# One feed-forward step of the odd chunks moved from slot 0 to slot 14 of the even chunk's middle

## What is computed

```python
x = L0_xattn(x, ctx, ctx, bias, bias, ...)   # 16 heads, 64 context tokens, layer norm
# L1 block
h1 = ln(x);  x = attn(h1, h1, 8-bit rounded q, k, v and weights) @ wo + bo + x    # 1024 keys
h2 = ln(x);  x = attn(h2, ctx, 8-bit rounded q, k, v and weights) @ wo + bo + x   # 64 keys
h3 = ln(x)
a, g = split(h3 @ ff_w1 + ff_b1)             # 2048 columns each
x = a * gelu(g) @ ff_w2 + ff_b2 + x
```

## Time and profile before

| | before |
| --- | --- |
| median of 3 runs | 3263.64 us (3263.4 to 3265.72) |
| the profiled execution, its own time | 3268.94 us |
| its span, first to last instruction | 3267.1 us |
| mean granted TensorE clock | 0.937 of full |
| TensorE matmul busy | 2906.6 us, 89% |
| VectorE busy | 2171.1 us, 66% |
| POOL busy | 1775.2 us, 54% |
| ScalarE busy | 1468.4 us, 45% |

### The profile page before, as it was taken

How to read it: one execution, slowest core, us unless ns; L and a number is a source line. 1 busy time by engine, 2 the same in 40 slices (tenths; PEclk the granted TensorE clock), 3 DMA queues, 4 the chain that set the end, 5 groups by cost and what they waited for, 6 DMA issues and landing times.

```text
span 3267.1 us, 50805 instructions
## 1 busy us (share of the span) xinstructions
PE 2906.6 (89%) x19712; PEld 2128.6 (65%) x19712; DVE 2171.1 (66%) x3591; ACT 1468.4 (45%) x2130; POOL 1775.2 (54%) x1698
## 2 busy tenths in 40 slices
PE   6677786898899989899889999899989999899998
PEld 6565554556677656667677656666767756666777
DVE  3467696784665686796675587687574588688521
ACT  5332462673333364474323365375324266275321
POOL 3456484785555185485455186386364277377321
PEclk9888756999999999999999999899999999999999
DMA  8744103335443314324443412333453322232444
GB/s 266 251 180 161 51 16 116 118 122 200 167 167 120 135 40 155 127 98 157 131 178 99 161 53 106 127 111 146 141 186 116 148 78 100 89 143 93 166 168 155
DMA packets 199758, 436.40 MB, mean 134 GB/s; under 512 B 94944, under 2 KB 103392, under 8 KB 182368
## 3 DMA queue, kind: packets, MB, share of 16 engines
q1 hardware_dynamic: 199520, 433.15, 37.1%
HBM read 363.38 MB, written 65.54 MB: 131 GB/s over the span
## 4 chain that ended last, share of the span: by engine, by line
PE 58%; POOL 16%; DVE 11%; issue 6%; ACT 4%; DMA 2%; SPq 1%; POOLq 0%; DVEq 0%; ACTq 0%
PE psum L1756 17%; PE psum L1758 15%; PE psum L1757 15%; POOL w1b L1011 6%; PE psum L2052 4%; PE psum L2040 2%; POOL rec L1006 2%; DVE e L1644 2%; PE psum L2066 1%; POOL u_lo L1030 1%; POOL x L925 1%; POOL fw_lo L1018 1%; ACT e L1315 1%; POOL w_lo L913 1%; DMA fw_lo<-pieces 1%
## 5 line engine op out<-in xcount | busy, mean ns | idle before, releaser
L1315 ACT ACTIVATE e<-e,nb 128x1024 f32<-128x1024 f32 x512 | 588.3, 1149 | 335.0 <-DVE e L1644 331.8
L1644 DVE TENSOR_SCALAR_CACHE_REDUCE e<-psum,nscale 128x1024 f32<-128x1024 f32 x512 | 652.8, 1278 | 76.8 <-POOL w1b L1011 54.4
L1011 POOL TENSOR_SCALAR w1b<-e,rec 128x1024 f16<-128x1024 f32 x512 | 574.6, 1122 | 95.2 <-POOL rec L1006 56.5
L1756 PE MATMUL psum<-h_hi,fw_hi 128*128 128x512 f32 x1024 | 458.1, 447 | 39.8 <-DVE h_lo L1401 14.8
L1657 DVE TENSOR_SCALAR w1T<-psum 128x1024 bf16<-128x1024 f16 x512 | 352.1, 688 | 96.6 <-PE psum L2052 93.1
L2052 PEld LDWEIGHTS psum<-ident,w1b 128*128 128x128 f16 x4096 | 255.8, 104 | 243.9 <-issue 131.5
L2052 PE MATMUL psum<-ident,w1b 128*128 128x128 f16 x4096 | 347.1, 233 | 74.9 <-POOL w1b L1011 46.1
L1757 PE MATMUL psum<-h_lo,fw_hi 128*128 128x512 f32 x1024 | 410.8, 401 | 0.0
L1758 PE MATMUL psum<-h_hi,fw_lo 128*128 128x512 f32 x1024 | 410.7, 401 | 0.0
L919 POOL TENSOR_TENSOR rstd<-ve,mhalf 128x1 f32<-128x1 f32 x128 | 88.5, 691 | 401.4 <-DVE ve L1507 401.4
L1756 PEld LDWEIGHTS psum<-h_hi,fw_hi 128*128 128x128 f32 x1024 | 196.3, 192 | 158.9 <-issue 98.4
(11 more groups left out here) (187 smaller groups left out, 6192.6 us busy)
## 6 DMA issues: line engine op xcount, KB each, us to landing
fw_hi<-pieces SPq DMA_DIRECT2D x168, 512.0 KB, 3.3
fw_lo<-pieces SPq DMA_DIRECT2D x168, 512.0 KB, 4.3
w_hi<-kept SPq DMA_DIRECT2D x45, 1024.0 KB, 4.9
w_lo<-kept SPq DMA_DIRECT2D x45, 1024.0 KB, 7.2
mixed<-mixed SPq DMA_DIRECT2D x32, 1024.0 KB, 5.1
fbias<-in_fside_Bx16xSxS SPq DMA_DIRECT2D x64, 256.0 KB, 3.0
unsplit<-in_L_xattn_ff_w SPq DMA_DIRECT2D x24, 512.0 KB, 5.0
pieces<-fw_hi SPq DMA_DIRECT2D x24, 512.0 KB, 2.7
```

What stands on the lines that cost most here:

```text
L1011: pool.tensor_scalar(w1b[u % NH][:], e1[u % NE][:], rec1[:, u % 8:u % 8 + 1], HALF, ALU.mult, ALU.add).then_inc(w1_ready.sem, 1)
L1315: act.activation(e1[s % NE][:], e1[s % NE][:], ACT.Exp, bias=nb1[:, s % NE:s % NE + 1], scale=-1.0, accum_out=sum1[:, s % 8:s % 8 + 1]).th ...
L1644: emptied_bank(dve.tensor_scalar(e1[s % NE][:], psum[:, i:i + 2, :].rearrange("p i n -> p (i n)"), nscale[:, 0:1], LARGEST, ALU.mult, ALU.min,
L1756: pe.matmul(o, s_hi, m_hi, start=first, stop=False)
```

## The change

In the list of the middle's slots for `FROM_A`, slot 0 is taken out and slot 14 put in. There are 14 steps in the middle, as before.

```diff
-FROM_A = host_quarters(8, 18, (0, 1, 2, 3, 4, 6, 10, 11, 12, 13, 15, 17, 19, 21))
+FROM_A = host_quarters(8, 18, (1, 2, 3, 4, 6, 10, 11, 12, 13, 14, 15, 17, 19, 21))
```

## The result

| | before | after |
| --- | --- | --- |
| median of 5 runs | 3263.64 us (3262.29 to 3267.55) | 3279.8 us (3276.44 to 3281.66) |
| the profiled execution, its own time | 3268.94 us | 3279.31 us |
| its span | 3267.1 us | 3277.5 us |
| mean granted TensorE clock | 0.937 | 0.937 |

A forecast was written before the change was run, and what follows sets the result against it. TensorE, busy 89% of the span, was taken as the bound. Terms -0.7 + 4.5 + 0.3 + 1.0 gave +5.1 us a middle, +15.3 for three: 3284.2 us profiled, less 5.3, is 3279.0 us, range 3269 to 3287.

The forecast's parts named there:

- (1): Even middle's entry, slot 0: TensorE idles 2.1 us for the split, yet the first output projection starts earlier; -0.7 us.
- (2): Slot 14: a3[3] runs wholly within TensorE's 6.15 us of idle time before the second turning; costs 0.
- (3): Slot 15: d3[0] waits for POOL's `u_lo`, now behind tile 3's scaling and 16-bit copy; +4.5 us, the main term.
- (5): Entry: the clock may fall after the new idle time, slowing a step and a projection; +1.0 us, ends 0 and 2.9.
- (4): Around slot 15: the clock is low when d3[0] starts, perhaps somewhat longer; +0.3 us, ends -1.9 and +1.5.
- (6): SP's load queues: pieces for a3[2] and d3[0] are issued later but arrive in time; 0 us, other end 2 us late.
- Rival A: Around slot 15: `u_lo` precedes tile 3's scaling and the clock stays high; 7.8 us faster, 3255.8 us; 6%.
- Rival B: Next self-attention's entry: its 1.88 us of idle time absorbs part of the delay; 3269.3 us with no clock loss; 10%.
- C: More than forecast: a3[2]'s piece lands 2 us late, or the clock is low at both places for long; 3286.5 us; 10%.
- D: Slot 14: the step doesn't fit and pushes the turning as well, because of the bank; 3287.7 us; 3%.

The follow-up runs named there:

- Experiment 7: The kernel before with slot 0's step moved into the self-attention (19 hosted steps there, 13 in the middle); ratio 1.0029.
- Experiment 6: The kernel before with a self-attention step (17 left there) put into slot 14 and d3[0] in slot 16; 3262.61 us, ratio 0.9989.
- experiment 4: The changed kernel with POOL's `u_lo` of a3[3] ahead of its scaling of tile 3 in the even middles; 3278.61 us, ratio 1.0034.
- experiment 1: The kernel before with slot 13's step moved to slot 14, slot 0 keeping its step; 3275.96 us, ratio 1.0028.
- experiment 2: The changed kernel with d3[0] moved from slot 15 to slot 16, behind the turning of tile 2; 3263.84 us, ratio 0.9994 to the kernel before.
- experiment 9: The kernel before with slot 1's step moved to slot 14, d3[0] staying in slot 15; 3270.0 us, ratio 1.0008.
- experiment 5: The changed kernel with nine unread matmuls in the entry's idle time; 3279.68 us, ratio 1.0037 to the kernel before.
- experiment 8: The kernel before with slot 1's step moved to slot 14 and d3[0] in slot 16; 3256.44 us, ratio 0.9975.

## Why the prediction was right

Forecast +15.3 us, 3279.0 us; measured 3279.8 us. By its steps, for each middle:

- **(1) The entry**, -0.7 us: measured -0.5 (2.28 us idle, not 2.1; the projection starts 0.25 us after `ht_lo` ends, where I took 0.1). Experiment 7 shows the same 2.28.
- **(2) Slot 14**, 0: measured 0.1 in chunk 4, where the clock didn't fall: 59.56 us to the second turning against 59.50. Experiment 6 shows a step more at no cost.
- **(3) The wait**, +4.5 us: measured +4.47 in all three. That POOL's order makes it is shown by experiment 4 (1.7 us back from that alone), and that it makes the kernel slower by experiments 1 and 2, and by experiment 9 in the middles. It does so because slot 0's step gives nothing back, terms (1) and (5); the 2.7 us a middle of slot 1's step would have paid for more than half of it (experiment 9).
- **(4) The clock around d3[0]**, +0.3 us, between -1.9 and +1.5: measured +0.4, -0.5 and +0.7 up to the turning of tile 2, and in chunk 2 another +0.4 behind it.
- **(5) The clock at the entry**, +1.0 us: measured +1.65, 0 and +1.65, mean 1.1. It is all or nothing at a place, and I forecast its mean. One of the two neighbours was read too narrowly. There is a fourth odd middle, chunk 1's, where TensorE idles 2.49 us before the second turning, at 849.10 us, and the granted clock is 0.51 for the 3.4 us behind it. So even in the odd middles the clock doesn't always stay high.
- **(6) The queues**, 0: no wait for a piece was seen. Here SP issues the loads for a3[2] after slot 10, and a3[2] starts without a wait for them (its idle time of 1.40 us ends with `gate`, as in the earlier trace rows).

The sum is 5.5 us a middle against 5.1 forecast. That the time agrees to 1 us is partly luck: the ratio's interval is 7.5 us wide, and the middles' 16.5 us stand against 10.4 us in the two profiled spans. Two terms, the clock's, were guesses between far ends, and their means came out near.

Rival A (clock kept high) failed where it was said to: `u_lo` came behind tile 3's scaling, and the clock was at 0.50 when d3[0] started. Rival B (the delay taken back at the next self-attention's entry) had the price of the forecast's low end, so only the trace can rule it out. It does: after the change TensorE idles 1.88 us at that entry in all three places, the same as in the earlier trace rows, and up to there the time from the turning of tile 2 is the same or longer. Of C the clock part came in mild form, D not at all.

The Trainium skill, page "TensorE: Matmul & The Clock Gate", section "HAM oscillation — how this bites in real kernels", says it takes long idle gaps to throw the clock back. The trace doesn't agree for this place: over the four profiled kernels with this entry uncovered (the change, experiments 2, 4 and 7) the clock fell at 7 of 12 gaps of 2.28 us. With the entry covered by a step it fell at none of 18 such places, and with the gap filled (experiment 5) at none of 3. So by the measurements short gaps can do it too.

## What to carry to other kernels

When a step is put into an idle gap, follow its result to its consumer: here the gap was real and the step in it free, but the next step in the list needs the result, and its producer on another engine fell behind 3 us of that engine's own work. Move the consumer with it (experiment 2), and take the step from a place where the engine has other work ready (experiment 8), not from one where it covers a wait. Both moves together turned +0.40% into -0.25%.

## What was not expected

- The same self-attention with the same 18 hosted steps takes 143.1 to 145.8 us, by its mean granted clock. That spread is as large as what a hosted step is worth there (1.9 to 2.4 us for the eighteenth), so two such stretches are compared at the same clock. Why the clock differs from one execution to the next isn't shown. Nor is why the nineteenth step cost 3.4 us or more in one of three places.
- The same idle gap of 2.28 us, in one execution, lowered the granted clock at chunks 2 and 6 and not at chunk 4, and cost 1.65 us where it did. What decides it wasn't found.
- Filling that gap with unread matmuls kept the clock high and shortened the middles by 5.2 us, but the kernel's measured time didn't show it.
